# Sums of two groups of a step in one run of 48 products, with a timetable of blocks on 50 partitions and a comparison in fp16 pairs

## The reference

```python
h = x @ W_in + b_in                      # 256 wide
for l in range(L):                       # L = 3
    agg = jax.ops.segment_sum(h[src], dst, num_segments=N) / deg
    logits = jnp.concatenate([h, agg], axis=-1) @ router_W[l] + router_b[l]
    vals, idx = jax.lax.top_k(logits, TOPK)
    gates = jax.nn.softmax(vals, axis=-1)
    weak = relu(einsum('nh,ehf->nef', agg, weak_W[l]) + weak_b[l])        # 4 experts
    sh = relu(einsum('nh,ehf->nef', agg, strong_W1[l]) + strong_b1[l])    # 4 experts, 512 wide
    strong = einsum('nef,efh->neh', sh, strong_W2[l]) + strong_b2[l]
    h = h + sigmoid(h @ conf_W[l] + conf_b[l]) * einsum('ne,neh->nh', gate_dense, experts)
```

## Time and profile before

| | us |
|---|---|
| median of 3 runs | 8308.41 |
| lowest, highest | 8306.09, 8310.05 |
| profiled execution, own time | 8296.74 |
| its span, first to last instruction | 8294.9 |
| PE, DVE, ACT, POOL busy, share of the span | 82%, 48%, 25%, 40% |
| three edge passes of Layer1, by POOL's gathers | 4267.6 |
| mean granted clock of TensorE, share of full speed | 0.846 |

### The profile page before, as it was taken

One profiled execution on the slowest core, in us unless ns is written; L12 is line 12 of the kernel. 1 busy time (PEld: TensorE's weight loads), 2 busy tenths in 40 slices (PEclk: granted clock), 3 DMA queues, 4 the chain that ended last, 5 costly groups with the idle time before them and its releaser, 6 DMA issues. The chain is left out here.

```text
span 8294.9 us, 149947 instructions
## 1 busy us (share of the span) xinstructions
PE 6806.2 (82%) x51092; PEld 4987.8 (60%) x51092; DVE 3941.9 (48%) x11483; ACT 2108.0 (25%) x6166; POOL 3355.4 (40%) x3406
## 2 busy tenths in 40 slices
PE   3999858888886888888688888867677676989899
PEld 1555546777775776777577777755555553545455
DVE  7777634444443444444355554546666662112111
ACT  3555412222221222222233333322222221000000
POOL 0000055555554555555455555536666661000000
PEclk6999979999997999999899999985555557999999
DMA  5344355454544444455444444434444445656565
GB/s 149 110 147 117 124 151 143 141 143 142 146 138 138 139 141 137 140 145 142 134 141 141 137 139 138 138 89 124 127 125 128 125 125 186 198 171 196 175 203 162
DMA packets 714970, 1188.63 MB, mean 143 GB/s; under 512 B 258881, under 2 KB 512997, under 8 KB 712162
## 3 DMA queue, kind: packets, MB, share of 16 engines
q0 software_dynamic: 200640, 601.97, 26.2%
q1 hardware_dynamic: 466786, 447.42, 18.0%
q10 hardware_dynamic: 46784, 129.65, 4.4%
HBM read 993.57 MB, written 185.20 MB: 142 GB/s over the span
## 5 line engine op out<-in xcount | busy, mean ns | idle before, releaser
L546 POOL DMA_INDIRECT ring<-parts,src_idx x2496 | 2453.7, 983 | 1948.1 <-PE sums L696 749.9
L1198 PEld LDWEIGHTS hid<-agg,big 128*128 128x128 f32 x9408 | 1157.1, 197 | 124.6 <-issue 88.1
L1198 PE MATMUL hid<-agg,big 128*128 128x128 f32 x9408 | 1184.7, 281 | 45.8 <-issue 27.3
L2346 PE MATMUL agg_ps<-sheet,big 128*128 128x448 f16 x6174 | 1193.6, 353 | 34.7 <-DMA sheet<-adj 34.7
L1159 PE MATMUL y<-big,strong 128*128 128x256 f32 x4704 | 1143.2, 390 | 37.3 <-issue 27.9
L546 POOL DMA_INDIRECT ring<-rows_yh,src_idx x832 | 839.5, 1009 | 556.8 <-issue 326.3
L1159 PEld LDWEIGHTS y<-big,strong 128*128 128x128 f32 x4704 | 868.8, 192 | 155.7 <-issue 50.1
L666 DVE TENSOR_TENSOR acc<-acc,sums 128x128 f32 x624 | 180.0, 289 | 1634.4 <-DMA acc<-in_edge_type 1116.1
L2346 PEld LDWEIGHTS agg_ps<-sheet,big 128*128 128x128 bf16 x6174 | 605.0, 99 | 581.7 <-DMA sheet<-adj 37.4
L1082 ACT ACTIVATE strong<-hid,s_b 128x128 f32<-128x128 f32 x2352 | 668.2, 369 | 916.5 <-PE hid L1198 625.4
L696 PE MATMUL sums<-onehot,ring 128*128 128x64 bf16 x14976 | 627.7, 196 | 320.5 <-issue 254.5
(11 more groups left out here) (370 smaller groups left out, 8529.5 us busy)
## 6 DMA issues: line engine op xcount, KB each, us to landing
sheet<-adj SPq DMA_DIRECT2D x294, 784.0 KB, 4.2
ring<-parts,src_idx POOLq DMA_INDIRECT x2496
adj<-big ACTq DMA_DIRECT2D x7, 5488.0 KB
...
```

The costliest lines, as they stand in the source:

```text
L546: nc.gpsimd.indirect_dma_start(ring[:, k, 0:YH] if edge_net else ring[:, k, :], None, table, bass.IndirectOffsetOnAxis(ap=src_idx[:, i * R ...
L1198: ins = nc.tensor.matmul(p["hid"][:, bank_at, j * P:(j + 1) * P], w["s1"][:, k, e, j * P:(j + 1) * P], s["agg"][:, k, :], start=(k == 0), ...
L2346: last = nc.tensor.matmul(ps[:, g % 2, 0:HALF_COLS], now[:, b, c, :], sheet[:, k, s * HALF_COLS:(s + 1) * HALF_COLS], start=(b == 0 and c ...
```

## The change

There are three edits.

**Pairs of groups.** A step's groups are paired in order, (0, 1), (2, 3), and a fifth or third one is single. PE sums no group of a pair until the slot of the second one's end, and then both in one run of 48 products, into the two banks, with tiles_done given behind each 24. DVE adds both there in a row (pair_sums) and makes the next one-hots behind the two adds. The edge network's pass stays as it was.

**The timetable.** The same numbers are worked out with blocks or steps on the partitions. PE spreads the row of first nodes (minr) over 50 partitions by a product with ones; one instruction compares and multiplies, one takes the maximum; PE turns the column to a row, DVE scans it, PE spreads it again over 49 partitions, and so on: four trips to PE (semaphores asked and spread) in place of the instructions on one partition and 2450 elements.

**The comparison.** gmax is copied to fp16, each value twice, and the thresholds are fp16 too; the comparison of 128x12544 elements then has fp16 operands whose innermost dimension is a pair.

```diff
+PAIRS = [tuple(range(FIRST_GROUP[i] + g, FIRST_GROUP[i] + min(g + 2, STEP_GROUPS[i])))
+         for i in range(STEPS) for g in range(0, STEP_GROUPS[i], 2)]
+PAIR_AT_END = {pair[-1]: pair for pair in PAIRS}
+SECOND = {pair[1] for pair in PAIRS if len(pair) > 1}
...
-                        own(nc.vector.tensor_tensor(touch, minr.unsqueeze(1).to_broadcast([1, NB, STEPS]),
-                                                    endr.unsqueeze(2).to_broadcast([1, NB, STEPS]), ALU.is_le))
-                        own(nc.vector.tensor_tensor(touch, touch, stepr.unsqueeze(1).to_broadcast([1, NB, STEPS]), ALU.mult))
-                        own(nc.vector.tensor_reduce(lastr, touch, AX.X, ALU.max))
-                        own(nc.vector.tensor_tensor(lastr, lastr, br, ALU.subtract))
+                        nc.vector.tensor_scalar(spare_less, iota_row0[0:STEPS, 0:NB], float(-SPARE_BLOCK), None, ALU.add
+                                                ).then_inc(asked, 1)
+                        dve.wait_ge(spread, 1)
+                        own(nc.vector.scalar_tensor_tensor(out=touch, in0=ip[0:NB, 0, 0:STEPS], scalar=end_col[0:NB, :],
+                                                           in1=iota_row0[0:NB, 0:STEPS], op0=ALU.is_le, op1=ALU.mult))
+                        own(nc.vector.tensor_reduce(last_col, touch, AX.X, ALU.max))
+                        nc.vector.tensor_tensor(last_col, last_col, iota_col0[0:NB, :], ALU.subtract).then_inc(asked, 1)
+                        own(nc.vector.tensor_scalar(mayber, mayber, float(2 * STEPS), 1.0, ALU.mult, ALU.add))
+                        dve.wait_ge(spread, 2)
+                        own(nc.vector.tensor_copy(lastr, ip[0:1, 1, 0:NB]))
                         own(nc.vector.tensor_tensor_scan(timer, lastr, lastr, 0.0, ALU.max, ALU.max))
-                        own(nc.vector.tensor_tensor(timer, timer, br, ALU.add))
-                        own(nc.vector.tensor_scalar(mayber, mayber, float(2 * STEPS), 1.0, ALU.mult, ALU.add))
-                        own(nc.vector.tensor_scalar(timer, timer, mayber, None, ALU.add))
-                        own(nc.vector.tensor_tensor(hit, timer.unsqueeze(1).to_broadcast([1, STEPS, NB]),
-                                                    stepr.unsqueeze(2).to_broadcast([1, STEPS, NB]), ALU.is_equal))
-                        own(nc.vector.tensor_reduce(tailr, hit.rearrange("o s b -> o (s b)"), AX.X, ALU.add))
-                        own(nc.vector.tensor_copy(tail_start[0:1, :], tailr))
-                        own(nc.vector.tensor_scalar(br, br, float(-SPARE_BLOCK), None, ALU.add))
-                        own(nc.vector.tensor_tensor(hit, hit, br.unsqueeze(1).to_broadcast([1, STEPS, NB]), ALU.mult))
-                        own(nc.vector.tensor_reduce(blockr, hit, AX.X, ALU.add))
-                        nc.vector.tensor_scalar(step_block[0:1, :], blockr, float(SPARE_BLOCK), None, ALU.add)
+                        own(nc.vector.tensor_tensor(timer, timer, block_no, ALU.add))
+                        nc.vector.tensor_scalar(timer, timer, mayber, None, ALU.add).then_inc(asked, 1)
+                        dve.wait_ge(asked, 3)
+                        own(nc.vector.tensor_scalar(in_steps, timer, float(STEPS), None, ALU.is_lt))
+                        own(nc.vector.tensor_reduce(tailr, in_steps, AX.X, ALU.add))
+                        nc.vector.tensor_copy(tail_start[0:1, :], tailr)
+                        dve.wait_ge(spread, 3)
+                        own(nc.vector.scalar_tensor_tensor(out=hit, in0=ip[0:STEPS, 2, 0:NB], scalar=step_no, in1=spare_less,
+                                                           op0=ALU.is_equal, op1=ALU.mult))
+                        nc.vector.tensor_reduce(block_col, hit, AX.X, ALU.add).then_inc(asked, 1)
+                        dve.wait_ge(spread, 4)
+                        nc.vector.tensor_scalar(step_block[0:1, :], ip[0:1, 3, 0:STEPS], float(SPARE_BLOCK), None, ALU.add)
...
+                        pe.wait_ge(asked, 1)
+                        nc.tensor.matmul(ip[0:NB, 0, 0:STEPS], ones[0:1, 0:NB], minr, start=True, stop=True).then_inc(spread, 1)
+                        pe.wait_ge(asked, 2)
+                        nc.tensor.transpose(ip[0:1, 1, 0:NB], last_col, ident[0:NB, 0:NB]).then_inc(spread, 1)
+                        pe.wait_ge(asked, 3)
+                        nc.tensor.matmul(ip[0:STEPS, 2, 0:NB], ones[0:1, 0:STEPS], timer, start=True, stop=True).then_inc(spread, 1)
+                        pe.wait_ge(asked, 4)
+                        nc.tensor.transpose(ip[0:1, 3, 0:STEPS], block_col, ident[0:STEPS, 0:STEPS]).then_inc(spread, 1)
...
-                            if q == 0 and g % 2 == 0:
+                            n = i * GROUPS + g
+                            if g % 2 == 0 and q == (GROUP - 1 if not edge_net and n in SECOND else 0):
+                                if q:
+                                    pair_sums(n)
                                 one_hots(i + g // 2, 1 - g // 2)
+                                if q:
+                                    return
...
-                            w = dve.value_load(win[0:1, bass.ds(i * GROUPS + g, 1)], min_val=0, max_val=SPARE)
-                            dve.wait_ge(tiles_done, i * RING + (GROUP * (g + 1) + RING))
-                            dve.wait_ge(added, i * GROUPS + (g + 2))
-                            nc.vector.tensor_tensor(
-                                acc[:, 0:n_sums, bass.ds(w, WIN)], acc[:, 0:n_sums, bass.ds(w, WIN)],
-                                sums[:, g % 2, 0:n_sums * WIN].rearrange("p (a j) -> p a j", j=WIN),
-                                ALU.add).then_inc(added, 1)
+                            pair_sums(n)
+                        def pair_sums(end):
+                            for n in PAIR_AT_END.get(end, ()):
+                                w = dve.value_load(win[0:1, bass.ds(n, 1)], min_val=0, max_val=SPARE)
+                                dve.wait_ge(tiles_done, GROUP * (n + 1) + RING)
+                                dve.wait_ge(added, n + 2)
+                                nc.vector.tensor_tensor(
+                                    acc[:, 0:n_sums, bass.ds(w, WIN)], acc[:, 0:n_sums, bass.ds(w, WIN)],
+                                    sums[:, n % 2, 0:n_sums * WIN].rearrange("p (a j) -> p a j", j=WIN),
+                                    ALU.add).then_inc(added, 1)
...
-                            if k % HALF == 0:
-                                pe.wait_ge(onehot_ready, i * 2 + (k // HALF + 1))
-                            if q == 0:
-                                pe.wait_ge(added, i * GROUPS + (g + 1))
-                            burst = width == H
-                            if burst and q < GROUP - 1:
+                            if q < GROUP - 1:
                                 return
-                            for j in range(k - q if burst else k, k + 1):
-                                pe.wait_ge(gathered[j], i * 16 + 16)
+                            for n in PAIR_AT_END.get(i * GROUPS + g, ()):
+                                group_sums(n)
+                        def group_sums(n):
+                            pe.wait_ge(onehot_ready, n // 2 + 1)
+                            pe.wait_ge(added, n + 1)
+                            g = n % GROUPS
+                            for q in range(GROUP):
+                                j = g * GROUP + q
+                                pe.wait_ge(gathered[j], n // GROUPS * 16 + 16)
                                 hot = onehot[:, g // 2, j % HALF, :]
                                 for a in range(width // D):
                                     for c in range(PARTS):
                                         lo = c * width + a * D
-                                        last = tile_sum(sums[:, g % 2, a * WIN:(a + 1) * WIN], ring[:, j, lo:lo + D],
-                                                        hot, j % GROUP == 0 and a == 0 and c == 0, j % GROUP == GROUP - 1)
-                            if q == GROUP - 1:
-                                last.then_inc(tiles_done, GROUP)
+                                        last = tile_sum(sums[:, n % 2, a * WIN:(a + 1) * WIN], ring[:, j, lo:lo + D],
+                                                        hot, q == 0 and a == 0 and c == 0, q == GROUP - 1)
+                            last.then_inc(tiles_done, GROUP)
...
-                        nc.vector.tensor_tensor(small, gmax[:, :].unsqueeze(2).to_broadcast([P, fine, TINY_BLOCKS]),
-                                                blocks[:, :].unsqueeze(1).to_broadcast([P, fine, TINY_BLOCKS]),
-                                                ALU.is_lt).then_inc(compared, 1)
+                        own(nc.vector.tensor_copy(gmax2[:, :, :], gmax[:, :].unsqueeze(2).to_broadcast([P, fine, 2])))
+                        nc.vector.tensor_tensor(small.rearrange("p g (b t) -> p g b t", t=2),
```

(3 more changed lines are left out.)

25 lines of the change are left out of this document (11 added, 14 removed).

## The result

The changed kernel takes 8721.55 us (median of 4 runs, 8713.52 to 8723.35) against 8307.25 for the kernel before: ratio 1.0494, interval 1.0478 to 1.0511. It is 414 us slower; 8237 was forecast, within 8040 to 8440.

A forecast was written before the change was run, and what follows sets the result against it. PE and POOL wait for each other, PE's sums notices being held while POOL issues gathers. Profiled 8296.7 less 15.3 (timetable), 6.4 (comparison) and 50 (pairs) is 8225; with 11.7 for the runs' median, 8237 us, range 8040 to 8440.

The forecast's parts named there:

- (c): Two legs: first, into a five's first pair, 12.2 us; second, from there to its second pair, 12.4; both within POOL's stretch.
- (d): Second pair of a five, through its single group, to the next step: 22.8 us, taken from one trace row.
- rival 2: Slow: hp's signal, falling late in POOL's stretch, is held in a third of steps of four; 8403 us, chance 0.27.
- (b): Second pair of a four to the next four's first pair: 14.9 us, where PE's work alone is 13.2.
- its extra block work, 38 us, stays: Third pass's 38 us above the other two passes, kept unchanged, cutting the pairs' gain from 88 to 50 us.
- (a): First to second pair of a step of four: 12.2 us, set by POOL's eight gathers, against 8.6 of PE work.
- The cycle: Steps of four, four, four and five in a pass, 17 groups: legs together 113.8 us, against 116.3 before.
- The list of passes: Times expected in the profile after for the three Layer1 passes: about 1381, 1381 and 1419 us.
- part 1: Pairs of groups in the three Layer1 passes: POOL gathers in stretches of eight, saving 50 us of waits.
- Rival 3: POOL misses the second notice 0.70 us after the first and gathers in fours; pairs gain nothing, 8287 us, chance 0.13.
- Rival 1: Fast: PE keeps its pace beside POOL's gathers, saving another 180 us in three passes; 8057 us, chance 0.15.
- Parts 2 and 3: Setup's timetable, saving 15.3 us, and the fp16 comparison in edge_codes(), saving 6.4 us.

## Why the prediction was wrong

- **What bounds the kernel** was read rightly: PE and POOL in a loop of held notices. Without gathers the kernel with single runs falls from 8285.62 to 7271.49 us on a slow chip.
- **The step that failed: legs (c) and (d)**, "Both end within a stretch: 12.2, and 12.4" and "I take it as it is", 22.8. Measured in the first pass: 13.7, 16.3 and 26.2. The sum took PE's block work as work that PE can do while POOL issues, and the hold as a matter of the sums' notices for POOL and DVE. But PE's own next product waits for ACT and DVE, they wait for PE's notices, and these are held too (up1's 8 us late, 4.86 us of idle PE; the ups' lateness 210 us before, 877 after). The text on rival 2 had just this mechanism for hp; it was not applied to the ups and the router. In (d) one row of before, in which hp got through, stood for a leg whose end depends on how POOL's next stretches fall.
- **Leg (b)**, 14.9: 15.7, 16.2, 20.9. In the first two passes it was mis-sized by about 1 us. In the third the step "its extra block work, 38 us, stays" failed: the third pass grew by 256 us (1704.5 against 1448.1), and in the rows above weak0's and the router's notices are late ahead of the ups, and up0 runs at a clock of 0.57.
- **Leg (a)**, "POOL's, 12.2 us": 12.3, 12.2 and 12.9, right. It is POOL's, and for that reason dear: PE alone needs 8.5.
- **Size of the misses.** In the first pass, leg by count: second (c) 43 us, (d) 37, (b) 19, first (c) 16, (a) 3. In the third: (b) 145, (d) 61, second (c) 46, first (c) 40, (a) 24. The cycle, 113.8 in the forecast, measured 124.4, 123.4 and 141.2 us (3 a + 2 b + c + c + d).
- **The list of passes** in the forecast, 1381, 1381 and 1419, doesn't agree with its own sum: the -50 of part 1 stands for some 1393, 1393 and 1431. Measured: 1509.3, 1498.2 and 1704.5.
- **Rival 2** had the right side and the right kind of mechanism, but its price, 8403, hung on one notice, hp's, and that one is no later than before (326 us in sum in both). Of the signs it named, a clock under 0.88 came in the third pass alone (0.89, 0.89, 0.87), and hp stood 5.6 us or more into a stretch in 25 of 118 steps. **Rival 3** did not happen: gathers stand in eights behind the pairs, both notices were caught (POOL starts at 1223.81, and its last gather of eight is at 1232.55). **Rival 1**: on the quick chips PE does keep its pace, but there the kernel before does too, and the pairs bring next to nothing.
- **The rule of the Trainium skill** ("SBUF — State Buffer", "SBUF: two separate sides": TensorE waits for nobody) agrees with the quick chips, where PE was busy 1051 of 1081 us beside POOL's gathers. On the others PE was busy 1204 of 1509 us, and what the rows show late there are notices. PE's slow pace in the earlier trace rows has no late notice in front of it; no run here shows whether a read of SBUF is slower there or something else.
- **Parts 2 and 3**: 21.7 forecast, 21.6 measured, with 15 to 32 in the interval; by the profile it is 22.3, so the agreement to 0.1 is luck. The setup gained 16.0 (SP's first transfer of the next stage at 40.19 instead of 56.21) where 15.3 was forecast: the timetable's chain ended at 38.75, 1.3 us ahead of the 40.0 forecast, so that SP's wait for x_first, to 39.3 as read in the earlier trace rows, now ended the phase. The comparison gained 6.3 with its copy (13.22 less 6.69 and 0.20) against 6.4.

Timetable and comparison without the pairs, 8285.62 us, is the version that beats both kernels on the slow kind of chip, the one before by 0.3%. On the quick kind it was not run by itself; the kernels there with the same steps, all gathers and no rest of POOL (7051 to 7060) are 0.4% faster than the kernel before.
